# Attention masks spread over three engines, value products ahead of the flags' sum, rows placed in pieces

## What is computed

```
qkv = (x_merge @ W_qkv).reshape(B, Mn, 3, NUM_HEADS, HEAD_DIM)   # B = 16, Mn = 1097, 8 heads of 8
attn = jnp.einsum('bhqd,bhkd->bhqk', q, k) * SCALE
top_k = Mn // 8                                                   # 137
kth = jax.lax.top_k(attn, top_k)[0][..., -1:]
attn = jnp.where(attn >= kth, attn, -jnp.inf)
attn = jax.nn.softmax(attn, axis=-1)
x_attn = jnp.einsum('bhqk,bhkd->bhqd', attn, v)
...
restored = restored.at[bidx, 2 * unm_idx].set(src_unm_o)          # and two more placements of rows
full = jnp.zeros((B, N, C), x.dtype).at[bidx, reserve].set(restored)
```

## Time and profile before

| what | value |
|---|---|
| median of three runs | 10730.66 us |
| the profiled execution's own time | 10726.99 us |
| its span, first to last instruction | 10725.3 us |
| VectorE busy, share of the span | 8630.9 us, 80% |
| TensorE busy (matmul) | 8027.7 us, 75% |
| ScalarE busy | 7589.9 us, 71% |
| GpSimd busy | 2345.1 us, 22% |
| mean granted clock of TensorE | 0.645 of full speed |

### The profile page before, as it was taken

The page is one execution under the profiler, slowest core; times in us unless marked ns, Lnnn a source line. Parts: engine busy times, 40 slices in busy tenths (PEclk is TensorE's granted clock), DMA queues, the critical chain, the costliest instruction groups (busy, mean ns, idle before and its releaser), DMA issues. The chain is left out here.

```text
span 10725.3 us, 166394 instructions
## 1 busy us (share of the span) xinstructions
PE 8027.7 (75%) x45265; PEld 5243.5 (49%) x45265; DVE 8630.9 (80%) x26258; ACT 7589.9 (71%) x12361; POOL 2345.1 (22%) x1944
## 2 busy tenths in 40 slices
PE   6777688857768788787788787885766787543998
PEld 6666455534434444444444444443433444443887
DVE  7888566659999999999999999998988999553333
ACT  5767222239879999999999999997977899221222
POOL 4666221210000000000000000000000000576766
PEclk9999866656556666666666666665656666555555
DMA  3332011100000000000000000000000000442111
GB/s 107 90 90 84 22 24 27 27 25 14 17 13 18 15 20 18 15 19 19 15 18 19 16 18 18 16 19 13 16 15 13 16 16 15 93 106 69 50 54 38
DMA packets 669924, 352.17 MB, mean 33 GB/s; under 512 B 587281, under 2 KB 605680, under 8 KB 665056
## 3 DMA queue, kind: packets, MB, share of 16 engines
q1 hardware_dynamic: 607920, 242.84, 10.3%
q0 software_dynamic: 58624, 60.72, 2.1%
q10 hardware_dynamic: 2384, 37.11, 0.9%
HBM read 200.20 MB, written 147.72 MB: 32 GB/s over the span
## 5 line engine op out<-in xcount | busy, mean ns | idle before, releaser
L1185 PE MATMUL a_psT<-a_qt,a_kt 74*122 74x366 bf16 x3456 | 1563.7, 452 | 777.3 <-ACT a_pT L1266 622.8
L1350 DVE MAX8 a_near<-a_below 122x8 f32<-122x219 f32 (+1 forms) x5760 | 1768.8, 373 | 0.1
L1188 PEld LDWEIGHTS a_psT<-a_weigh,a_drops 122*122 122x122 bf16 x10368 | 1579.6, 191 | 210.0 <-issue 16.3
L1266 ACT ACTIVATE a_pT<-a_psT 122x732 f32<-122x732 f32 (+1 forms) x1920 | 1372.0, 715 | 361.9 <-PE a_psT L1188 345.2
L1343 DVE SCALAR_TENSOR_TENSOR a_below<-a_s,a_te,a_signs 122x1097 f32<-122x1097 f32 x1152 | 1547.1, 1353 | 79.0 <-remote 74.8
L1274 ACT ACTIVATE a_junk<-a_s,a_aim 122x1097 bf16<-122x1097 f32 x1152 | 1377.0, 1203 | 289.3 <-DVE a_s L1417 289.3
L1188 PE MATMUL a_psT<-a_weigh,a_drops 122*122 122x122 bf16 x10368 | 1532.8, 274 | 11.4 <-issue 11.4
L1201 PE MATMUL a_psO<-a_pT,a_v 122*32 122x366 f32 x6912 | 1409.3, 701 | 0.0
L1274 ACT ACTIVATE a_signs<-a_s,a_te 122x1097 bf16<-122x1097 f32 x1152 | 1401.9, 1220 | 4.9 <-DVE a_te L1335 4.9
L1274 ACT ACTIVATE a_junk<-a_s,a_te 122x1097 bf16<-122x1097 f32 x1152 | 1387.6, 1207 | 0.0
L1515 POOL DMA_DIRECT2D a_dst<-o x15 | 13.8, 918 | 6118.9 <-DMA o<-a_o 6118.9
(11 more groups left out here) (375 smaller groups left out, 14383.3 us busy)
## 6 DMA issues: line engine op xcount, KB each, us to landing
xbuf<-r_blank ACTq DMA_DIRECT2D x16, 1990.6 KB
e_xg<-xbuf SPq DMA_DIRECT2D x56, 568.8 KB, 4.1
r_bc<-pr SPq DMA_DIRECT2D x16, 1372.0 KB, 7.1
a_k<-kT SPq DMA_DIRECT2D x384, 51.5 KB
a_q<-qT SPq DMA_DIRECT2D x384, 51.5 KB
a_kt<-kT SPq DMA_DIRECT2D x384, 51.5 KB
a_qt<-qT SPq DMA_DIRECT2D x384, 51.5 KB
r_xt<-in_x SPq DMA_DIRECT2D x16, 784.0 KB
```

The source lines that it names most:

```text
L1185: pe.matmul(out[:, x, 0:CW], kt[q][:, u * QP:(u + 1) * QP], qt[q][:, c * CW:(c + 1) * CW], start=True, stop=False)
L1188: mm = pe.matmul(out[:, x, t * QP:(t + 1) * QP], drops[:, c * CT + t, u * QP:(u + 1) * QP], weigh[:, :], start=False, stop=t == CT - 1)
L1266: act.activation(pT[j % RING][:, 0:w, :], psT[(q + j) % 2][:, 0:w, 0:CW], ACT.Exp).then_inc(exped, 1)
L1350: mx = dve.max(near[:, t, g, :], below[t % 3][:, EDGES[g]:EDGES[g + 1]])
```

## The change

VectorE masks one tile (`OWN` = 1), ScalarE four (`BY_ACT` = 4), GpSimd the last four, each in two operations: the score is taken from the threshold, then clipped between 0 and `BIG`. `raw` signals a semaphore of its own, `chosen`, for which ScalarE waits in place of `flagged`. All 15 slots of fills and value products come ahead of the flags' sum. VectorE reads the flags behind its only mask, copies the aim ahead of `order`, and normalises one tile earlier. `EXP_SPAN` goes from 18 to 17. The placing of an image's rows is cut into pieces that GpSimd issues behind its masks in five successive steps, from two small copies of the row lists. A reordering of semaphore declarations in `rank`, the new semaphores and buffers (`under`, `gids`, `toks`) and an optional `behind` in `steps` are left out here.

```diff
-LATE_SLOTS = 3
-OWN = 4
-EXP_SPAN = 18
+OWN = 1
+BY_ACT = 4
+BY_POOL = QT - OWN - BY_ACT
+EXP_SPAN = 17
...
                 low, high = score_banks(t)
                 pe.matmul(low[:, 0:HALF], q_, ks[o][:, 0:HALF], start=True, stop=True).then_inc(scored, 1)
-                if t == 0 and last:
-                    for i in range(SLOTS - LATE_SLOTS + 1, SLOTS):
-                        slot(s - 2, p, i)
...
                     if CT * (c + 1) > OWN:
-                        wait(pe, act_masked, (QT - OWN) * h + CT * (c + 1) - OWN)
+                        wait(pe, act_masked, BY_ACT * h + min(BY_ACT, CT * (c + 1) - OWN))
+                    if CT * (c + 1) > OWN + BY_ACT:
+                        wait(pe, pool_masked, BY_POOL * h + CT * (c + 1) - OWN - BY_ACT)
...
-                for i in range(SLOTS - LATE_SLOTS):
+                for i in range(SLOTS):
...
-                if last:
-                    slot(s - 2, p, SLOTS - LATE_SLOTS)
-                for t in range(QT):
-                    if ahead:
+                if ahead:
+                    for t in range(QT):
                         score(s, p, o, t, now, late, last)
...
                     if late and n == 2 * QT:
-                        wait(act, flagged, 2 * s - 1)
-                        for m in range(OWN, QT):
+                        wait(act, chosen, s)
+                        for m in range(OWN, OWN + BY_ACT):
...
         @block.gpsimd
         def _(pool):
-            for b in range(B - 1):
-                pool.wait_ge(o_stored, 16 * (H // 2) * (b + 1))
-                place(pool, k, d, b, b, srcs, dsts, src_in, dst_in, put)
+            def step(s, p, old, last, late, now, ahead):
+                o = 1 - p
+                if late:
+                    wait(pool, flagged, 2 * s - 1)
+                    for m in range(OWN + BY_ACT, QT):
+                        if m == OWN + BY_ACT or m % CT == 0:
+                            wait(pool, filled, SLOTS * (s - 2) + PER * (m // CT + 1))
+                        n = m - OWN - BY_ACT
+                        wait(pool, pool_masked, BY_POOL * (s - 1) + n)
+                        apart(pool, k)
+                        pool.tensor_scalar(under[:, :], sc[o][:, m, :], -1.0, raw[:, m:m + 1], ALU.mult, ALU.add).then_inc(lowered, 1)
+                        wait(pool, lowered, BY_POOL * (s - 1) + n + 1)
+                        apart(pool, k)
+                        pool.tensor_scalar(drops[:, m, 0:MN], under[:, :], BIG, 0.0, ALU.min, ALU.max).then_inc(pool_masked, 1)
+
+            def behind(i, p):
+
+                if p == 2:
+                    pool.tensor_copy(gids[:, :], k.gidx[:, bass.ds((i - 1) * NS, NS)]).then_inc(listed, 1)
+                    pool.tensor_copy(toks[:, :], k.tokens[:, bass.ds(i - 1, 1), :, :].rearrange("p a i two -> p (a i two)")
+                                     ).then_inc(listed, 1)
+                elif p == 3:
+                    wait(pool, listed, 2 * i)
+                    wait(pool, o_stored, 16 * (H // 2) * i)
+                    apart(pool, k)
+                    pool.dma_start(dsts[:, :, :], d.o[bass.ds((i - 1) * MP, ND), :].rearrange("(i p) c -> p i c", p=TP)
+                                   ).then_inc(dst_in, 16)
+                    for j in range(NS):
+                        pool.indirect_dma_start(out=srcs[:, j, :], out_offset=None, in_=d.o,
...
+                elif p == 4:
+                    wait(pool, dst_in, 16 * i)
...
+                elif p == 5:
+                    wait(pool, src_in, 16 * NS * i)
...
+                elif p == 6:
+                    wait(pool, put, 16 * 2 * NS * i)
+                    apart(pool, k)
+
+            steps(pool, step, behind)
...
-                link.after(dve.tensor_tensor(raw[:, :], te[o][:, :], kth[:, :], ALU.add), 9)
+                dve.tensor_tensor(raw[:, :], te[o][:, :], kth[:, :], ALU.add).then_inc(chosen, 1)
...
                 wait(dve, masked, OWN * (s - 1) + min(t + 1, OWN))
-                if t >= OWN:
-                    wait(dve, act_masked, (QT - OWN) * (s - 1) + t + 1 - OWN)
+                if OWN <= t < OWN + BY_ACT:
+                    wait(dve, act_masked, BY_ACT * (s - 1) + t + 1 - OWN)
+                elif t >= OWN + BY_ACT:
+                    wait(dve, pool_masked, BY_POOL * (s - 1) + t + 1 - OWN - BY_ACT)
...
-                    if old and t == 2:
+                    if old and t == 1:
                         normalise(s, p)
...
-                if late:
-                    order()
-                    search(l, o)
                 if ahead:
                     stat = k.stat[:, bass.ds(s + 1, 1), 0, :].rearrange("p a t -> p (a t)")
                     dve.tensor_copy(aim[:, :], stat).then_inc(aimed, 1)
                 if late:
+                    order()
+                    search(l, o)
+                    wait(dve, chosen, s)
                     for t in range(OWN):
                         if t % CT == 0:
                             wait(dve, filled, SLOTS * (l - 1) + PER * (t // CT + 1))
                         dve.tensor_scalar(drops[:, t, 0:MN], sc[o][:, t, :], raw[:, t:t + 1], None, ALU.is_lt).then_inc(masked, 1)
-                        if t == OWN - 2:
-                            wait(dve, flag_sum, s)
-                            dve.tensor_copy(flag[:, :], psS[0:1, FLAG_AT:FLAG_AT + QT + 1]).then_inc(flagged, 1)
+                    wait(dve, flag_sum, s)
+                    dve.tensor_copy(flag[:, :], psS[0:1, FLAG_AT:FLAG_AT + QT + 1]).then_inc(flagged, 1)
```

More of the change, by code:

```diff
@@ L1072, in attend @@
         (scored, evacuated, aimed, windowed, flagged, flag_sum, settled, masked, act_masked, filled, exped, valued, o_out,
-         folded, normed, peaked, peak_turned, peak_cut, peak_stored, o_stored) = (sem("a_" + x) for x in (
+         chosen, pool_masked, listed, lowered, folded, normed, peaked, peak_turned, peak_cut, peak_stored, o_stored) = (sem("a_" + x) for x in (
              "scored", "evacuated", "aimed", "windowed", "flagged", "flag_sum", "settled", "masked", "act_masked", "filled",
-             "exped", "valued", "o_out", "folded", "normed", "peaked", "peak_turned", "peak_cut", "peak_stored",
+             "exped", "valued", "o_out", "chosen", "pool_masked", "listed", "lowered", "folded", "normed", "peaked", "peak_turned", "peak_cut", "peak_stored",
              "o_stored"))
@@ L1079, in attend @@
         srcs, dsts = (sb(x, [TP, NS, C]) for x in ("a_src", "a_dst"))
+        under = sb("a_under", [QP, MN])
+        gids, toks = sb("a_gids", [TP, NS], U32), sb("a_toks", [TP, 2 * NS], U32)
         src_in, dst_in, put = (sem("a_" + x) for x in ("src_in", "dst_in", "put"))
@@ L1086, in wait, with steps @@
                 eng.wait_ge(s, value)
-        def steps(eng, step):
+        def steps(eng, step, behind=None):
             def alone(s):
                 step(s, s % 2, *(0 <= s - back < HEADS for back in (3, 2, 1, 0, -1)))
+                if behind and H <= s < HEADS:
+                    behind(s // H, s % H)
             for s in range(-1, H):
@@ L1097, in steps @@
                     step(H * i + p, p % 2, True, True, True, True, True)
+                    if behind:
+                        behind(i, p)
             for s in range(HEADS - H, HEADS + 3):
@@ L1245, in step @@
                               stop=True).then_inc(flag_sum, 1)
-                if last:
-                    slot(s - 2, p, SLOTS - LATE_SLOTS)
-                for t in range(QT):
-                    if ahead:
+                if ahead:
+                    for t in range(QT):
                         score(s, p, o, t, now, late, last)
-                    elif last and t == 0:
-                        for i in range(SLOTS - LATE_SLOTS + 1, SLOTS):
-                            slot(s - 2, p, i)
             pe.wait_ge(k.started, 2)
@@ new lines, in behind @@
+            def behind(i, p):
[11 more added lines that the diff above has]
+                        pool.indirect_dma_start(out=srcs[:, j, :], out_offset=None, in_=d.o,
+                                                in_offset=bass.IndirectOffsetOnAxis(ap=gids[:, j:j + 1], axis=0)
+                                                ).then_inc(src_in, 16)
+                elif p == 4:
+                    wait(pool, dst_in, 16 * i)
+                    apart(pool, k)
+                    for j in range(NS):
+                        pool.indirect_dma_start(out=d.y, out_offset=bass.IndirectOffsetOnAxis(ap=toks[:, 2 * j + 1:2 * j + 2], axis=0),
+                                                in_=dsts[:, j, :], in_offset=None).then_inc(put, 16)
+                elif p == 5:
+                    wait(pool, src_in, 16 * NS * i)
+                    apart(pool, k)
+                    for j in range(NS):
+                        pool.indirect_dma_start(out=d.y, out_offset=bass.IndirectOffsetOnAxis(ap=toks[:, 2 * j:2 * j + 1], axis=0),
```

(10 more changed lines are left out.)

16 lines of the change are left out of this document (8 added, 8 removed).

## The result

The changed kernel takes 10391.81 us (median of 4 runs, 10374.2 to 10429.84), against 10733.83 us for the kernel before, measured beside it (4 runs). The ratio is 0.9682, with a 95% interval of 0.9654 to 0.9711: 3.2% or some 342 us faster. The profiled execution took 10374.2 us, 353 us less than the one of before, which the sum of the prediction is made against.

What follows compares the result with a forecast made beforehand. VectorE and ScalarE were taken as almost full in a 50.03 us step; VectorE's 47.3 us plus 0.3 us gave 47.6, saving 2.43 us over 127 steps: 10727 - 309 = 10418, 10420 against the runs. Range 10320 to 10780 us.

Steps and rivals of the forecast that it cites:

- The step before: Mean attention step of the kernel before, from the search's end: 2901.92 us over 58 steps, 50.03 us.
- VectorE's masks, four to one: VectorE's step behind the search: 3 x 0.70 = 2.1 us off, leaving 46.4 us of work before waits.
- Value products ahead of the flags' sum: TensorE's order at the search's end: a wait of 0.6 to 1.2 us replaces VectorE's 1.49 us.
- Normalise a tile earlier: VectorE's normalise: TensorE's wait before the transpose goes, and ScalarE's at the fill; ScalarE 46.4 to 47.4 us.
- GpSimd: Four tiles' masks on GpSimd: 1.10 us an instruction, 10.4 us in all, ending R+11.2, 1.5 us before needed.
- Rows placed in pieces: GpSimd's DMAs behind successive steps' masks: at most 10 us from R+11.2; uncovered, one piece would delay masks by 10 us.
- The sum: Whole attention step: VectorE 47.3 plus 0.3 us gives 47.6; 2.43 us saved in each of 127 steps, 309 us.
- The two-input rate: Rival on GpSimd's masks: 2.16 us an instruction, tile 8's read waits 7.0 us, 11270 us in all; chance 0.16.
- Turns throughout: Rival: VectorE cannot read scores while GpSimd works, step 56.1 us, 11500 us in all; chance 0.04.
- ScalarE keeps its waits: Rival: ScalarE stays the bound with its 2.5 us of waits, step 48.9 us, 10587 us in all; chance 0.2.
- nothing could be measured: Rival: GpSimd at 1.5 to 1.7 us an instruction gives back VectorE's saving, 10680 to 10780 us; chance 0.07.

## Why the prediction was right, and where it was off

The forecast was 10420 us and faster; 10391.81 us came, within the range. By its own steps:

- **The step before.** "58 steps later" was a miscount: 57, so 50.91 us and not 50.03. It drops out of the difference in good part, but it hid which engine would be full. The prediction's ScalarE, "50.0 - 2.5 - 1.1 = 46.4 us of work", is 47.3 with the right step, and 47.06 us is what the 62 steps show. Its VectorE would come to 50.9 - 1.5 - 2.1 = 47.3, and 48.2 with the new wait.
- **VectorE's masks, four to one.** 2.1 us were forecast, and VectorE's work fell by 2.3 us. Alone they are worth nothing, because the wait grew by as much; the prediction added the two parts and did not say that one needs the other.
- **Value products ahead of the flags' sum.** The mechanism held: the two groups of value products were the wait for the second half score. The new wait of "0.6 to 1.2 us" measured 1.10 us, near its upper end, so the first score is read at R+1.8 and not at "about 1.5 us after R"; by the runs it is the register load and branch, 1.01 us behind the cast in most steps, as the bound "to about 1.1 us" allowed. Whether the 0.41 us of before was a wait for a score at all is open: the run with the order and the old masks has it with the score long ready.
- **Normalise a tile earlier.** Right in mechanism (no transpose that waits, ScalarE's waits from 2.5 to 0.7 us a step), but it was costed at ScalarE's waits only. It also keeps the last exponential, and so the flags' sum, on time: in the new order it is worth 196 us, more than half of the whole gain. The span of 17, for which up to 1.0 us of waits was left, costs and brings nothing in the new order.
- **GpSimd.** 1.10 us an instruction was taken, 1.18 and 1.10 came, with the 0.20 us between them; the masks' end at R+11.2 is R+11.1, and tile 8's read at R+12.7 is R+12.6. VectorE's mask did win the first turn, by 0.4 us. That the end agrees so closely is in part chance: GpSimd started at R+0.4 and not at R+0.8, and its instructions took a little longer.
- **Rows placed in pieces.** No mask came late, as forecast. But the pieces are not what does it: behind the masks one piece fits as well. It takes 30.7 us there, because the 23.9 us of the earlier trace rows leave out the gaps of 0.3 us between the DMAs.
- **The sum.** The saving was put at 2.43 us a step and was 50.91 - 48.06 = 2.85. On VectorE it was added up from 2.1 us of masks, 0.6 us of waits for scores (1.49 less a middle of 0.9) and 0.3 us taken off for inputs handed over late. Measured were 2.30 us of work, 1.49 - 1.10 = 0.39 us of waits for scores and 0.16 us of other idle time. So the work was put 0.2 us too low and the new wait 0.2 us too short, which cancel; the difference is that other idle time and the 0.3 us, a loss that did not show. Forecast were 309 us over 127 steps; the mean steps over the whole of attention gave 343 us.
- **The rivals.** That ScalarE would be the fuller engine came, with 98% of a step, but without its waits of 2.5 us. The two-input rate fell with the first GpSimd row: 1.24 us in the mean is below the break-even of 1.63 us, and the run with half more work showed what lies beyond it. Turns throughout fell too: VectorE's reads out of PSUM took 0.69 us beside GpSimd, as before without it. That ScalarE keeps its waits did not come. In the run with normalise at its old place they are back at 128.2/71 = 1.8 us a step; that its 10594.63 us lie so near the 10587 us of that rival is chance, because there VectorE waits 68.3/71 = 1.0 us a step for the flags' sum as well. That nothing could be measured fell as well.

## What to carry to other kernels

Where two engines are both near full and a third carries results between them, price the edits together: lighter masks alone gave 0.3%, the order with its two shifts 1.7%, all together 3.2%. When work is moved to GpSimd, look at which VectorE instructions would run beside it: those with two inputs from SBUF and the mask from SBUF to SBUF were held here, reads out of PSUM were not, so GpSimd should wait until the last of the former has started. And count the steps between two rows before dividing: a miscount by one moved two engines' work by 0.9 us and hid which of them would be full.

## What the runs showed of the hardware

- GpSimd does a two-operation instruction with one tensor input and a scalar per partition on 122 x 1097 numbers in 1.18 us (f32 out), and with two constants in 1.10 us (bf16 out), near the rate of its copies in the earlier trace rows, with 0.20 us between dependent ones.
- Small VectorE instructions with two SBUF inputs were held to the end of a running GpSimd instruction: one on nine numbers a partition took 1.11 us instead of 0.17, one on five 1.05 us. Its reads out of PSUM were not held (0.69 us beside GpSimd and without it).
- Between the end of the flags' cast and the first VectorE instruction behind the branch on it lie 1.01 to 1.05 us in some six of eight steps and about 1.4 us in the others, both in the changed kernel and where VectorE's 0.80 us mask runs in between; without load and branch it is about 0.45 us in every step. The profile puts that time down to TensorE.
